# Two heads' scores in neighbouring PSUM banks, read by one instruction of 1024 columns, in the attention loop of a transformer kernel

## The chip, the cores and the metric
One core of a Trainium2 chip runs the whole program. TensorE multiplies and transposes, VectorE and ScalarE read its results out of PSUM (8 banks of 512 float32 columns in each of 128 partitions), GpSimd does small work. The metric is the device time of one execution in microseconds (us), lower is better; three runs give the median.

## The reference
Two transformer layers follow each other on x of 2 x 512 x 256: a linear attention, a mixture of 8 experts, then a softmax attention with grouped keys, and a second mixture. Each of the four parts works on a normalised x, is normalised and added to x. The change touches the third part only:

```python
# L1: 32 query heads, 8 key heads, width 8; x is viewed as batch 2, length 512 at this size
qkv = einsum('bsd,df->bsf', x, Wqkv) + bqkv
k, v = repeat(k, 4), repeat(v, 4)
scores = einsum('bqhd,bkhd->bhqk', q, k) / sqrt(8)
attn = softmax(scores, axis=-1)
out = einsum('bhqk,bkhd->bqhd', attn, v).reshape(b, s, 256) @ Wo + bo
```

## The kernel before
Every engine has its own instruction list, written out in Python, and they meet at semaphores. The attention loop works on NG = 16 groups (2 batches x 8 key heads), each with GH = 4 query heads, and each group takes TB = 4 steps of 128 rows. So there are STEPS = 64 steps c, and END = 73 turns of the loop with the drain.

The softmax needs a row's maximum before the exponentials, and the kernel makes the scores twice. In `scores1(c, i)` TensorE makes 128 queries x 512 keys per head; VectorE (`maximum`) takes each row's negated maximum into `mx`. GpSimd splits the maxima of a group into three bf16 parts and writes them as additional columns of the queries, so that the second product comes out with the maximum already subtracted. In `scores2(d, i)`, six steps later (d = c - LAG), TensorE makes 128 keys x 512 queries per head from `kT` and `qT2`, and ScalarE writes the exponentials into `pr`. `weigh(d - 2, half)` multiplies `pr` with the values into bank 6, for half of the columns at a time; the values have a column of ones that gives the sum.

A head has 32 rows of TensorE's array. Two heads of `scores1` (0, 1) and two of `scores2` (2, 3) are issued one after the other in the first half of a step, heads 2, 3 and 0, 1 in the second.

The order of a step on TensorE is `scores1(c, 0)`, `scores2(d, 0)`, `weigh(d-2, 0)`, a turn, `scores1(c, 1)`, `scores2(d, 1)`, perhaps a projection of the second batch (`project_qkv`, steps 4 to 7), `weigh(d-2, 1)`. A turn is four transposes through bank 7: at c % 4 = 0 of a finished group's output `oT` ("o"), at 1 of queries with their maxima ("q2"), at 2 of the next group's queries ("q1"), and at 3 in three of the steps of keys ("k"). ScalarE copies a turn to SBUF between its second and third exponential (q1, q2, k), or copies bank 6 to `oT` at the head of a step ahead of the "o" turn. In the first step of a group both halves of `weigh` come at the end of the step, behind `scores2(d, 1)`.

The banks: `scores1` goes round banks 0, 1, 2 (RING = 3), one head in each; `scores2` round banks 3, 4, 5. A score matmul waits until the reader has finished the bank's use three heads before: `max_read` counts VectorE's maxima, `exp_ready` ScalarE's exponentials. After step 64 only `scores2` is left, and the transposes and projection of the first batch's output (`turn_att`, `project`) are put between.

Two lines carry most of VectorE's and ScalarE's work in the loop:

```python
v.tensor_reduce(mx[n % 2][:, t, j:j + 1], s1_bank(c, j), AX.X, ALU.max, negate=True)   # L1481
nc.scalar.activation(pr[d % 3][:, j], s2_bank(d, j), ACT.Exp, scale=SCALE)              # L1256
```

On TensorE L1359 is `scores1`, L1374 `scores2`, L1389 `weigh`, L1343 a turn, L1315 a projection of queries, keys and values, L1406 and L1418 the output's transposes and projection.

Of the kernel before, what the change touches and what calls it, by code (L numbers as in the profile page):

```python
# [24 lines left out]
ALU = mybir.AluOpType  # L25
ACT = mybir.ActivationFunctionType
AX = mybir.AxisListType

P = 128
B, S, D = 2, 512, 256  # L30
NT = B * S // P
# [46 lines left out]
def build(nc, a, out):  # L78
    ctx = ExitStack()
    with ctx:  # L80
# [1058 lines left out]
        STEPS = NG * TB  # L1139
        LAG = 6  # L1140
        PROJ_AT = STEPS + 1
        PROJ_BANK = [ps[2]] * TB + ps[TB:NT]
        QKV_BANK = (4, 5, 6, 7, 3, 4, 6, 6)
        QKV_AT = 4
        RING = 3
        HEADS2 = (2, 3, 0, 1)
        AV_BANK, TURN_BANK = 6, 7

        def s1_bank(c, j):

            return ps[(c * GH + j) % RING]

        def s2_no(d, j):

            return d * GH + HEADS2.index(j)

        def s2_bank(d, j):

            return ps[RING + s2_no(d, j) % RING]

        def turns_at(c):

# [56 lines left out]
        def act_l1(act, turn_copy, complete):  # L1219
            def copy_turn(what):  # L1220
                kind, n = what
                act.wait_ge(turned, turn_no(what))
                dst = kT[n] if kind == "k" else (qT1 if kind == "q1" else qT2)[n % 2]
                nc.scalar.activation(dst[:], turn_bank(TURNS.index(what)), ACT.Copy).then_inc(turn_copied, 1)

            def hi_parts(b, t):

                act.wait_ge(qkv_ready, b * TB + t + 1)
                stack_hi(nc.scalar, b, t, "k").then_inc(k_hi_made[b], 1)
                stack_hi(nc.scalar, b, t, "q").then_inc(q_hi_made[b], 1)  # L1230

            act.wait_ge(l1_consts, L1_CONSTS)
            for t in range(TB):
                hi_parts(0, t)
            for what in FIRST:
                copy_turn(what)
            turn_copy(2, 2)
            turn_copy(2, 3)
            for c in range(END):
                d = c - LAG  # L1240
                if c == 1:
                    complete(1)
                n = (c - 12) // TB if c % TB == 0 and c >= 12 else -1
                if 0 <= n < NG:
                    act.wait_ge(av_done, (n + 1) * TB)
                    nc.scalar.activation(oT[:], ps[AV_BANK], ACT.Copy).then_inc(oT_ready, 1)
                if d >= 3 and d < STEPS:
                    act.wait_ge(av_done, d - 2)
                for i, j in enumerate(HEADS2):
                    if i == 2:  # L1250
                        for what in turns_at(c):
                            if what[0] != "o":
                                copy_turn(what)
                    if 0 <= d < STEPS:
                        act.wait_ge(s2_made, s2_no(d, j) + 1)
                        nc.scalar.activation(pr[d % 3][:, j], s2_bank(d, j), ACT.Exp, scale=SCALE).then_inc(exp_ready, 1)  # L1256
            for t in range(TB, NT):
                act.wait_ge(attT_made, t + 1)
                nc.scalar.activation(xT[:, :, t * P:(t + 1) * P],
                                     ps[t][:, 0:D].rearrange("p (c n) -> p c n", c=KC), ACT.Copy).then_inc(att1_copied, 1)  # L1260

        def pool_l1_loop(pool, link):
# [24 lines left out]
            for n in range(NG):  # L1287
                if 2 <= n < 2 + TB:
                    second_batch(n - 2)
                if n == 2 + TB:  # L1290
                    values(1)

                bb, gg = n // NKV, n % NKV
                pool.wait_ge(max_read, (n + 1) * TB * GH)
                m = mx[n % 2][:].rearrange("p t h -> p (t h)")
                low = [r[:].rearrange("p t h -> p (t h)") for r in mr]
                link(g.tensor_copy(mp[:, 0], m))  # L1297
                link(g.tensor_tensor(low[0], m, mp[:, 0], ALU.subtract))
                link(g.tensor_copy(mp[:, 1], low[0]))
                link(g.tensor_tensor(low[1], low[0], mp[:, 1], ALU.subtract))  # L1300
                link(g.tensor_copy(mp[:, 2], low[1]))
                g.tensor_copy(qs[bb][:, :, gg * GH:(gg + 1) * GH, MAXAT:MAXAT + MAXN],
                              mp[:].rearrange("p i (t h) -> p t h i", h=GH)).then_inc(max_ready, 1)

        def pe_l1(pe, turn_x):
# [3 lines left out]
            def project_qkv(t):  # L1309

                pe.wait_ge(xT_ready, 4 * 2 + t // 2 + 1)
                if t >= TB:
                    pe.wait_ge(qkv_ready, t if t == NT - 1 else TB)
                for c in range(KC):
                    last = mm(ps[QKV_BANK[t]][:, 0:QKV], xT[:, c, t * P:(t + 1) * P], wqkv[:, c],  # L1315
                              start=(c == 0), stop=(c == KC - 1))
                last.then_inc(qkv_made, 1)
# [28 lines left out]
            def scores1(c, i):  # L1346

                n, t = c // TB, c % TB
                if t == 0 and i == 0:
                    wait_read(pe, ("q1", n))  # L1350
                    wait_read(pe, ("k", n // GH))
                for j in (2 * i, 2 * i + 1):
                    k = c * GH + j
                    if k >= RING:
                        pe.wait_ge(max_read, k - RING + 1)
                    elif k == RING - 1:
                        pe.wait_ge(xT_ready, 4 * 2 + 4)
                    rows = slice(j * HW, (j + 1) * HW)
                    mm(s1_bank(c, j), qT1[n % 2][rows, t * P:(t + 1) * P], kT[n // GH][rows, :], start=True,  # L1359
                       stop=True).then_inc(s1_made, 1)  # L1360

            def scores2(d, i):

                n, kc = d // TB, d % TB
                if d == 0 and i == 0:
                    pe.wait_ge(qkv_ready, TB + 2)
                if kc == 0 and i == 0:
                    wait_read(pe, ("q2", n))
                for j in HEADS2[2 * i:2 * i + 2]:
                    k = s2_no(d, j)  # L1370
                    if k >= RING:
                        pe.wait_ge(exp_ready, k - RING + 1)
                    rows = slice(j * HW, (j + 1) * HW)
                    mm(s2_bank(d, j), kT[n // GH][rows, kc * P:(kc + 1) * P], qT2[n % 2][rows, :], start=True,  # L1374
                       stop=True).then_inc(s2_made, 1)

            def weigh(d, half):

                n, kc = d // TB, d % TB
                pe.wait_ge(exp_ready, (d + 1) * GH)  # L1380
                if half == 0 and kc == 0:
                    pe.wait_ge(vals_ready, n // NKV + 1)
                    if n == 0:
# [7 lines left out]
                if half:  # L1391
                    last.then_inc(av_done, 1)

            def turn_att(t):

                if t < TB:
                    pe.wait_ge(att_ready, NKV)
                    pe.wait_ge(max_read, GH * STEPS)
                    if t >= 2:
                        pe.wait_ge(att0_copied, t - 1)  # L1400
                    into = ps[t % 2]
                else:
                    pe.wait_ge(att_ready, NG)
                    into = ps[t]
                for c in range(KC):
                    last = nc.tensor.transpose(into[:, c * P:(c + 1) * P], xn[:, t, c * P:(c + 1) * P], ident[:])  # L1406
                last.then_inc(attT_made, 1)
# [19 lines left out]
            for c in range(END):  # L1427
# [4 lines left out]
                    scores2(d, 0)  # L1432
                if 0 <= d - 2 < STEPS and (d - 2) % TB:
                    weigh(d - 2, 0)
                for what in turns_at(c):
                    turn(what)
                if c < STEPS:
                    scores1(c, 1)
                if 0 <= d < STEPS:
                    scores2(d, 1)  # L1440
                if QKV_AT <= c < QKV_AT + TB:
# [14 lines left out]
        def dve_l1(dve, link, mark, settle, close_y, close_x):  # L1456
# [15 lines left out]
                    key_lo(t - 1)  # L1472
            key_lo(TB - 1)

            def maximum(c, j):

                n, t = c // TB, c % TB
                dve.wait_ge(s1_made, c * GH + j + 1)
                if t == 0 and j == 0 and n >= 2:
                    dve.wait_ge(max_ready, n - 1)  # L1480
                v.tensor_reduce(mx[n % 2][:, t, j:j + 1], s1_bank(c, j), AX.X, ALU.max, negate=True).then_inc(max_read, 1)  # L1481

            def outputs(n):

# [12 lines left out]
            def copy_att(t):  # L1497
                dve.wait_ge(attT_made, t + 1)
                v.tensor_copy(xT[:, :, t * P:(t + 1) * P],
                              ps[t % 2][:, 0:D].rearrange("p (c n) -> p c n", c=KC)).then_inc(att0_copied, 1)  # L1500

            for c in range(END):
                n = (c - 12) // TB if c % TB == 0 and c >= 12 else -1
                if c < STEPS:
                    for j in range(GH):
                        maximum(c, j)
                if QKV_AT <= c < QKV_AT + TB:
                    take(TB + c - QKV_AT)
                if 0 <= n < NG:
# [54 lines left out]
```

## Time and profile before

| | us |
|---|---|
| median of 3 runs (lowest, highest) | 715.25 (712.79, 715.26) |
| the profiled execution, whole time | 715.23 |
| its span from the first to the last instruction | 713.5 |
| TensorE busy in the span | 605.1 |
| VectorE, ScalarE, GpSimd busy | 398.5, 335.6, 207.2 |
| first maximum starts, last starts | 390.8, 574.5 |
| first exponential starts, last starts | 410.2, 593.6 |

The loop so takes the part of the span from about 390 to 597 us. Start times are counted from the beginning of the span. A duration of a matmul includes its way through the array, so that two matmuls one behind the other overlap in the records; the distance between starts is what one costs.

### The profile page before, as it was taken

To read this page: it belongs to the slowest core of one execution; us is meant where nothing else is said; L and a number is where in the kernel's file an instruction comes from. 1 tells how busy PE (TensorE), PEld (TensorE's weight loads), DVE (VectorE), ACT (ScalarE), POOL (GpSimd) and SP (SyncE) were. 2 spreads that over 40 slices of the span, in tenths; PEclk is the share of its full clock that TensorE was granted. 3 is DMA by queue.
4 is the path that set the end of the run, shared out by engine and by line. 5 is a ranking of instruction groups with operands and counts; after the bars stand their busy time and mean duration, and the time that the engine had idled before them with its cause. 6 is when DMAs were issued, how large, how long until landed. Compare 5 with 4: busy or idle time off the path is not lost.

```text
span 713.5 us, 11382 instructions
## 1 busy us (share of the span) xinstructions
PE 605.1 (85%) x4164; PEld 395.9 (55%) x4164; DVE 398.5 (56%) x906; ACT 335.6 (47%) x668; POOL 207.2 (29%) x307
## 2 busy tenths in 40 slices
PE   3975999999999884999916999999999998589980
PEld 2854888898788771556613444444444445246650
DVE  4331643652571485522265889889989936442225
ACT  5520432442341235222206288988988884523321
POOL 1695183074154002523333013201010101141331
PEclk9997999999999996899967699999999999699995
DMA  6000300120088009322330000000000000931213
GB/s 206 30 1 1 119 1 1 40 79 1 30 156 153 5 1 294 120 62 88 100 125 1 0 1 2 1 1 2 2 1 2 1 1 11 335 114 36 90 51 118
DMA packets 40773, 42.53 MB, mean 60 GB/s; under 512 B 7632, under 2 KB 36176, under 8 KB 40720
## 3 DMA queue, kind: packets, MB, share of 16 engines
q1 hardware_dynamic: 38512, 35.77, 17.7%
q0 software_dynamic: 2208, 6.04, 2.4%
q8 instruction: 34, 0.56, 0.3%
q14 instruction: 19, 0.16, 0.1%
HBM read 30.77 MB, written 11.03 MB: 59 GB/s over the span
## 4 chain that ended last, share of the span: by engine, by line
PE 70%; DVE 10%; POOL 7%; ACT 6%; DMA 4%; issue 2%; SPq 0%; ACTq 0%; POOLq 0%; DVEq 0%
PE psum L1359 9%; PE psum L1389 9%; PE psum L294 7%; PE psum L1085 7%; PE psum L296 7%; PE psum L295 7%; PE psum L1116 4%; PE psum L1343 4%; ACT pr L1256 3%; DVE stat L621 2%; POOL sorted_x L574 2%; PE psum L1315 2%; PE psum L938 2%; PE psum L1032 1%; PE psum L1374 1%
## 5 line engine op out<-in xcount | busy, mean ns | idle before, releaser
L1481 DVE TENSOR_REDUCE mx<-psum 128x1 f32<-128x512 f32 x256 | 158.9, 683 | 18.5 <-PE psum L1359 17.8
L1256 ACT ACTIVATE pr<-psum 128x512 f32<-128x512 f32 x256 | 138.9, 598 | 25.4 <-PE psum L1374 24.8
L1359 PE MATMUL psum<-kT,qT 32*128 32x512 f32 x256 | 81.5, 513 | 3.2 <-DVE mx L1481 1.9
L1389 PE MATMUL psum<-pr,vals 128*32 128x256 f32 x1024 | 77.9, 389 | 0.0
L1374 PE MATMUL psum<-qT,kT 32*128 32x512 f32 x256 | 66.1, 492 | 0.2 <-DVE qkv L1463 0.2
L910 ACT ACTIVATE sg<-psum 128x256 f32<-128x256 f32 x46 | 17.7, 384 | 97.3 <-PE psum L1085 62.6
L1359 PEld LDWEIGHTS psum<-kT,qT 32*128 32x128 f32 x256 | 35.3, 188 | 50.4 <-issue 23.8
L805 DVE TENSOR_TENSOR h<-sg,psum 128x256 f32<-128x256 f32 x46 | 19.3, 421 | 72.9 <-ACT sg L910 72.9
L938 PE MATMUL psum<-ident,xn_id 128*128 128x128 f32 x64 | 15.7, 406 | 49.9 <-ACT xn_id L848 49.8
L1085 PE MATMUL psum<-w_gu,xgT 128*128 x120 | 56.4, 592 | 0.0
L580 POOL DMA_INDIRECT routed_y<-yr,xg x30 | 28.9, 962 | 84.3 <-DVE yr L813 84.3
L500 POOL TENSOR_TENSOR rstd<-var,mhalf 128x4 f32<-128x4 f32 x16 | 16.8, 1051 | 108.4 <-DVE nmean L628 108.4
L1297 POOL CAST mp<-mx 128x16 bf16<-128x16 f32 x16 | 3.2, 198 | 154.6 <-DVE mx L1481 154.6
L885 ACT ACTIVATE q_hi<-q 128x512 fp32r<-128x512 f32 x32 | 20.2, 633 | 48.3 <-DVE q L747 48.3
L879 ACT ACTIVATE q<-psum 128x512 f32<-128x512 f32 x32 | 19.1, 597 | 49.9 <-PE psum L296 49.9
L938 PEld LDWEIGHTS psum<-ident,xn_id 128*128 128x128 f32 x64 | 8.7, 188 | 56.5 <-ACT xn_id L848 45.2
L552 POOL TENSOR_TENSOR ksum_t<-k_hi 128x1024 f32<-128x1024 f32 x8 | 19.2, 2395 | 69.0 <-DVE k_lo L716 69.0
L1389 PEld LDWEIGHTS psum<-pr,vals 128*32 128x32 f32 x1024 | 22.1, 108 | 29.9 <-ACT pr L1256 18.8
L294 PE MATMUL psum<-kvo_hi,q_hi 128*128 128x256 f32 x128 | 37.5, 293 | 0.7 <-DVE q_lo L695 0.7
L721 DVE TENSOR_TENSOR nk<-psum,same_head 128x8 f32<-128x8 f32 x16 | 1.9, 162 | 63.0 <-PE psum L1010 63.0
L296 PE MATMUL psum<-kvo_hi,q_lo 128*128 128x256 f32 x128 | 36.2, 283 | 0.0
L295 PE MATMUL psum<-kvo_lo,q_hi 128*128 128x256 f32 x128 | 36.2, 282 | 0.0
(201 smaller groups left out, 1386.2 us busy)
## 6 DMA issues: line engine op xcount, KB each, us to landing
w_gu<-in_L_ffn_gate_w SPq DMA_DIRECT2D x16, 256.0 KB, 6.1
w_gu<-in_L_ffn_up_w SPq DMA_DIRECT2D x16, 256.0 KB, 6.4
w_d<-in_L_ffn_down_w SPq DMA_DIRECT2D x16, 256.0 KB, 6.4
xg<-sorted_x SPq DMA_DIRECT2D x30, 128.5 KB, 2.2
sorted_x<-zeros SPq DMA_DIRECT2D x30, 128.0 KB, 5.1
wk_f<-in_L_attn_Wk SPq DMA_DIRECT2D x4, 512.0 KB, 5.1
wq_f<-in_L_attn_Wq SPq DMA_DIRECT2D x4, 512.0 KB, 5.9
wv_f<-in_L_attn_Wv SPq DMA_DIRECT2D x4, 512.0 KB, 3.7
```

What stands on the lines that cost most here:

```text
L294: nc.tensor.matmul(o, lhs[0], rhs[0], start=start, stop=False, **kw)
L295: nc.tensor.matmul(o, lhs[0], rhs[1], start=False, stop=False, **kw)
L296: return nc.tensor.matmul(o, lhs[1], rhs[0], start=False, stop=stop, **kw)
L580: g.indirect_dma_start(routed_y[l][:, :], bass.IndirectOffsetOnAxis(ap=xg[r % NXG][:, D:D + 1].bitcast(U32), axis=0), yr[r % 4][:], None). ...
L938: last = nc.tensor.transpose(ps[i if p else 4 + i][:, c * 256 + t % 2 * P:c * 256 + (t % 2 + 1) * P], xn[:, t, c * P:(c + 1) * P], ident[:])
L1085: last = mm(ps[2 + u % 2][:], xgT[r % 2][:, c], w_gu[:, bass.ds(experts[r], 1), c, :], start=(c == 0), stop=(c == KC - 1))
L1116: last = mm(ps[6 + u % 2][:, 0:D], hT[u % 2][:, c], w, start=(c == 0), stop=(c == FC - 1))
L1256: nc.scalar.activation(pr[d % 3][:, j], s2_bank(d, j), ACT.Exp, scale=SCALE).then_inc(exp_ready, 1)
L1359: mm(s1_bank(c, j), qT1[n % 2][rows, t * P:(t + 1) * P], kT[n // GH][rows, :], start=True, stop=True).then_inc(s1_made, 1)
L1374: mm(s2_bank(d, j), kT[n // GH][rows, kc * P:(kc + 1) * P], qT2[n % 2][rows, :], start=True, stop=True).then_inc(s2_made, 1)
L1389: last = mm(ps[AV_BANK][j * VW:(j + 1) * VW, cols], vals[:, n // NKV * TB + kc, n % NKV // GH * GH + j, :], pr[d % 3][:, j, cols], start=( ...
L1481: v.tensor_reduce(mx[n % 2][:, t, j:j + 1], s1_bank(c, j), AX.X, ALU.max, negate=True).then_inc(max_read, 1)
```

## The change
The scores of two heads are put side by side in two neighbouring banks, and one instruction reads both: a maximum over 128 x (2, 512), giving two columns of `mx`, and an exponential over 1024 columns. Both kinds of score share banks 0 to 5, as three pairs of banks: the list PAIRS has the pairs in TensorE's order (s1, s2, s1, s2 in a full step; only s1 in steps 0 to 5), and pair k has place k % 3 and waits until the pair last in its place has been read. Behind the last s1 the s2 pairs alternate between places 1 and 2. `max_read` and `exp_ready` count pairs. The turn is issued behind `scores1(c, 1)` instead of ahead of it, and ScalarE copies it between its two exponentials. The projection's banks 3, 4 for tiles 4, 5 become bank 6, each waiting for the addition of the tile before; the output's transposes use bank 0 alone, its projection bank 1.

```diff
-        PROJ_BANK = [ps[2]] * TB + ps[TB:NT]
-        QKV_BANK = (4, 5, 6, 7, 3, 4, 6, 6)
+        PROJ_BANK = [ps[1]] * TB + ps[TB:NT]
+        QKV_BANK = (4, 5, 6, 7, 6, 6, 6, 6)
...
-        RING = 3
-        HEADS2 = (2, 3, 0, 1)
+        HEADS1, HEADS2 = (0, 2), (2, 0)
...
+        PAIRS = []
+        for c_ in range(STEPS + LAG):
+            for i_ in range(2):
+                if c_ < STEPS:
+                    PAIRS.append(("s1", c_, i_))
+                if c_ >= LAG:
+                    PAIRS.append(("s2", c_ - LAG, i_))
+        IN_TURN = PAIRS.index(("s1", STEPS - 1, 1)) + 1
+        PLACE = [k_ % 3 if k_ < IN_TURN else 1 + (k_ - IN_TURN) % 2 for k_ in range(len(PAIRS))]
+
+        def pair_bank(what):
+
+            first = 2 * PLACE[PAIRS.index(what)]
+            return psum[:, first * 512:(first + 2) * 512]
+
+        def pair_no(step, i):
+
+            return 2 * step + i + 1
+
+        def wait_pair(pe, what):
+
+            k = PAIRS.index(what)
+            for kind, step, i in [PAIRS[k_] for k_ in range(k) if PLACE[k_] == PLACE[k]][-1:]:
+                pe.wait_ge(max_read if kind == "s1" else exp_ready, pair_no(step, i))
...
                 for i, j in enumerate(HEADS2):
-                    if i == 2:
+                    if i == 1:
                         for what in turns_at(c):
                             if what[0] != "o":
                                 copy_turn(what)
                     if 0 <= d < STEPS:
-                        act.wait_ge(s2_made, s2_no(d, j) + 1)
-                        nc.scalar.activation(pr[d % 3][:, j], s2_bank(d, j), ACT.Exp, scale=SCALE).then_inc(exp_ready, 1)
+                        act.wait_ge(s2_made, 2 * pair_no(d, i))
+                        nc.scalar.activation(pr[d % 3][:, j:j + 2].rearrange("p h n -> p (h n)"),
+                                             pair_bank(("s2", d, i)), ACT.Exp, scale=SCALE).then_inc(exp_ready, 1)
...
-                    pe.wait_ge(qkv_ready, t if t == NT - 1 else TB)
+                    pe.wait_ge(qkv_ready, t)
...
+                wait_pair(pe, ("s1", c, i))
+                for v in range(2):
+                    j = HEADS1[i] + v
                     rows = slice(j * HW, (j + 1) * HW)
-                    mm(s1_bank(c, j), qT1[n % 2][rows, t * P:(t + 1) * P], kT[n // GH][rows, :], start=True,
-                       stop=True).then_inc(s1_made, 1)
-
+                    last = mm(pair_bank(("s1", c, i))[:, v * S:(v + 1) * S], qT1[n % 2][rows, t * P:(t + 1) * P],
+                              kT[n // GH][rows, :], start=True, stop=True)
+                    last.then_inc(s1_made, 1)
...
                 if 0 <= d - 2 < STEPS and (d - 2) % TB:
                     weigh(d - 2, 0)
+                if c < STEPS:
+                    scores1(c, 1)
                 for what in turns_at(c):
                     turn(what)
-                if c < STEPS:
-                    scores1(c, 1)
                 if 0 <= d < STEPS:
                     scores2(d, 1)
...
-                v.tensor_reduce(mx[n % 2][:, t, j:j + 1], s1_bank(c, j), AX.X, ALU.max, negate=True).then_inc(max_read, 1)
+                v.tensor_reduce(mx[n % 2][:, t, HEADS1[i]:HEADS1[i] + 2],
+                                pair_bank(("s1", c, i)).rearrange("p (h n) -> p h n", h=2), AX.X, ALU.max,
+                                negate=True).then_inc(max_read, 1)
```

## Rows read from the trace of the kernel before

**Rows 1.** The page, chain that ended last: shares of the span by engine.
```profile
PE 70%; DVE 10%; POOL 7%; ACT 6%; DMA 4%; issue 2%; SPq 0%; ACTq 0%; POOLq 0%; DVEq 0%
```

**Rows 2.** Busy time by stretch: length, engines' busy us (instructions), then clock, DMA, GB/s.
```profile
393.00:396.00 3.00, 3.00 (x6) 1.32 (x6) 3.00 (x6) 1.31 (x4) 0.00 (x0) 0.50 0.00 0
...
404.00:406.00 2.00, 2.00 (x5) 0.62 (x3) 0.29 (x1) 0.00 (x0) 0.00 (x0) 0.52 0.00 0
...
486.50:497.80 11.30, 10.72 (x113) 4.96 (x116) 10.30 (x18) 10.02 (x19) 1.25 (x7) 1.00 0.01 1
```

**Rows 3.** Timeline of TensorE in one step: start, length, instructions merged.
```profile
480.10 0.66 PE L1343 MATMUL psum<-ident,qs 128*128 128x128 f32 x4
480.69 0.50 PE L1359 MATMUL psum<-kT,qT 32*128 32x512 f32 x2
480.69 0.50 PE L1374 MATMUL psum<-qT,kT 32*128 32x512 f32 x2
481.12 0.64 PE L1389 MATMUL psum<-pr,vals 128*32 128x256 f32 x8
481.69 0.77 PE L1359 MATMUL psum<-kT,qT 32*128 32x512 f32 x2
481.97 0.50 PE L1374 MATMUL psum<-qT,kT 32*128 32x512 f32 x2
```

**Rows 4.** Timelines of VectorE and ScalarE in the same group.
```profile
481.22 4.88 DVE L1481 TENSOR_REDUCE mx<-psum 128x1 f32<-128x512 f32 x8 [0.48 <-PE psum L1359]
...
482.59 2.22 ACT L1256 ACTIVATE pr<-psum 128x512 f32<-128x512 f32 x4 [0.21 <-PE psum L1374]
484.69 0.60 ACT L1246 ACTIVATE oT<-psum 128x512 f32<-128x512 f32 x1
```

**Rows 5.** Groups by form, whole span: busy us, mean ns of one, idle before.
```profile
L1481 DVE TENSOR_REDUCE mx<-psum 128x1 f32<-128x512 f32 x256 | 158.9, 683 | 18.5 <-PE psum L1359 17.8
L1256 ACT ACTIVATE pr<-psum 128x512 f32<-128x512 f32 x256 | 138.9, 598 | 25.4 <-PE psum L1374 24.8
...
L747 DVE TENSOR_TENSOR q<-q,psum 128x512 f32<-128x512 f32 x32 | 21.8, 680 | 0.6 <-PE psum L1037 0.4
...
L805 DVE TENSOR_TENSOR h<-sg,psum 128x256 f32<-128x256 f32 x46 | 19.3, 421 | 72.9 <-ACT sg L910 72.9
...
L910 ACT ACTIVATE sg<-psum 128x256 f32<-128x256 f32 x46 | 17.7, 384 | 97.3 <-PE psum L1085 62.6 <-PE psum L1078 34.7
```

**Rows 6.** The chain in order of time: a projection; output turns of five groups.
```profile
411.32 1.50 PE psum L1315 x4
...
428.48 0.63 PE psum L1343 x4
...
462.40 0.63 PE psum L1343 x4
...
474.15 0.63 PE psum L1343 x4
...
485.44 0.63 PE psum L1343 x4
...
575.78 0.63 PE psum L1343 x4
```

**Rows 7.** Timeline of TensorE, start of the loop: steps 4, 6 and 8.
```profile
402.74 2.93 PE L1315 MATMUL psum<-wqkv,xT 128*128 128x384 f32 x4
...
408.92 0.50 PE L1359 MATMUL psum<-kT,qT 32*128 32x512 f32 x2
...
417.73 1.07 PE L1389 MATMUL psum<-pr,vals 128*32 128x256 f32 x16
```

**Rows 8.** Timeline of TensorE, end of the loop, steps 65 and 66.
```profile
577.76 0.49 PE L1374 MATMUL psum<-qT,kT 32*128 32x512 f32 x2
...
581.71 0.74 PE L1374 MATMUL psum<-qT,kT 32*128 32x512 f32 x2
...
582.38 0.64 PE L1389 MATMUL psum<-pr,vals 128*32 128x256 f32 x8
```

More of the change, by code:

```diff
@@ L1141, in build @@
         PROJ_AT = STEPS + 1
-        PROJ_BANK = [ps[2]] * TB + ps[TB:NT]
-        QKV_BANK = (4, 5, 6, 7, 3, 4, 6, 6)
+        PROJ_BANK = [ps[1]] * TB + ps[TB:NT]
+        QKV_BANK = (4, 5, 6, 7, 6, 6, 6, 6)
         QKV_AT = 4
-        RING = 3
-        HEADS2 = (2, 3, 0, 1)
+        HEADS1, HEADS2 = (0, 2), (2, 0)
         AV_BANK, TURN_BANK = 6, 7
[L1149 to L1159, printed above, removed]
+        PAIRS = []
[16 more added lines that the diff above has]
+                pe.wait_ge(max_read if kind == "s1" else exp_ready, pair_no(step, i))
         def turns_at(c):
@@ L1293, in pool_l1_loop @@
                 bb, gg = n // NKV, n % NKV
-                pool.wait_ge(max_read, (n + 1) * TB * GH)
+                pool.wait_ge(max_read, (n + 1) * TB * 2)
                 m = mx[n % 2][:].rearrange("p t h -> p (t h)")
@@ L1351, in scores1 @@
                     wait_read(pe, ("k", n // GH))
[L1352 to L1357, printed above, removed]
+                if (c, i) == (0, 1):
+                    pe.wait_ge(xT_ready, 4 * 2 + 4)
+                wait_pair(pe, ("s1", c, i))
+                for v in range(2):
+                    j = HEADS1[i] + v
                     rows = slice(j * HW, (j + 1) * HW)
-                    mm(s1_bank(c, j), qT1[n % 2][rows, t * P:(t + 1) * P], kT[n // GH][rows, :], start=True,
-                       stop=True).then_inc(s1_made, 1)
+                    last = mm(pair_bank(("s1", c, i))[:, v * S:(v + 1) * S], qT1[n % 2][rows, t * P:(t + 1) * P],
+                              kT[n // GH][rows, :], start=True, stop=True)
+                    last.then_inc(s1_made, 1)
             def scores2(d, i):
                 n, kc = d // TB, d % TB
-                if d == 0 and i == 0:
-                    pe.wait_ge(qkv_ready, TB + 2)
                 if kc == 0 and i == 0:
                     wait_read(pe, ("q2", n))
[L1369 to L1372, printed above, removed]
+                wait_pair(pe, ("s2", d, i))
+                for v in range(2):
+                    j = HEADS2[i] + v
                     rows = slice(j * HW, (j + 1) * HW)
-                    mm(s2_bank(d, j), kT[n // GH][rows, kc * P:(kc + 1) * P], qT2[n % 2][rows, :], start=True,
-                       stop=True).then_inc(s2_made, 1)
+                    last = mm(pair_bank(("s2", d, i))[:, v * S:(v + 1) * S], kT[n // GH][rows, kc * P:(kc + 1) * P],
+                              qT2[n % 2][rows, :], start=True, stop=True)
+                    last.then_inc(s2_made, 1)
             def weigh(d, half):
                 n, kc = d // TB, d % TB
-                pe.wait_ge(exp_ready, (d + 1) * GH)
+                pe.wait_ge(exp_ready, (d + 1) * 2)
                 if half == 0 and kc == 0:
@@ L1392, in weigh, with wait_place0 @@
                     last.then_inc(av_done, 1)
+            def wait_place0(pe):
+                kind, step, i = [x_ for x_, at_ in zip(PAIRS, PLACE) if at_ == 0][-1]
+                pe.wait_ge(max_read if kind == "s1" else exp_ready, pair_no(step, i))
             def turn_att(t):
@@ L1397, in turn_att @@
                     pe.wait_ge(att_ready, NKV)
[L1398 to L1401, printed above, removed]
+                    pe.wait_ge(max_read, 2 * STEPS)
+                    if t:
+                        pe.wait_ge(att0_copied, t)
+                    else:
+                        wait_place0(pe)
+                    into = ps[0]
                 else:
@@ L1473, in dve_l1, with maximum @@
             key_lo(TB - 1)
-            def maximum(c, j):
+            def maximum(c, i):
                 n, t = c // TB, c % TB
-                dve.wait_ge(s1_made, c * GH + j + 1)
-                if t == 0 and j == 0 and n >= 2:
+                dve.wait_ge(s1_made, 2 * pair_no(c, i))
+                if t == 0 and i == 0 and n >= 2:
                     dve.wait_ge(max_ready, n - 1)
-                v.tensor_reduce(mx[n % 2][:, t, j:j + 1], s1_bank(c, j), AX.X, ALU.max, negate=True).then_inc(max_read, 1)
+                v.tensor_reduce(mx[n % 2][:, t, HEADS1[i]:HEADS1[i] + 2],
+                                pair_bank(("s1", c, i)).rearrange("p (h n) -> p h n", h=2), AX.X, ALU.max,
+                                negate=True).then_inc(max_read, 1)
             def outputs(n):
@@ L1499, in copy_att @@
                 v.tensor_copy(xT[:, :, t * P:(t + 1) * P],
-                              ps[t % 2][:, 0:D].rearrange("p (c n) -> p c n", c=KC)).then_inc(att0_copied, 1)
+                              ps[0][:, 0:D].rearrange("p (c n) -> p c n", c=KC)).then_inc(att0_copied, 1)
             for c in range(END):
@@ L1504, in dve_l1 @@
                 if c < STEPS:
-                    for j in range(GH):
-                        maximum(c, j)
+                    for i in range(2):
+                        maximum(c, i)
                 if QKV_AT <= c < QKV_AT + TB:
```

## The prediction
> **What bounds the kernel now.** I read the chain that ended last first: 70% of it is TensorE, 10% VectorE, 6% ScalarE [rows 1], so a microsecond taken off VectorE or ScalarE counts only where TensorE waits for it. Then the table of stretches for one group of four steps (11.30 us): TensorE is busy 10.72, VectorE 10.30 and ScalarE 10.02, at a granted clock of 1.00, TensorE's upper level of 2.4 GHz [rows 2]. Three engines are nearly full, so the order of the work decides. Last I read the timeline of one step for the prices of TensorE's pieces, start to start [rows 3]. The turn of four transposes takes 0.59 (480.10 to 480.69). The first score pair and the second start together at 480.69, on different rows of the array, and the weighing starts at 481.12, so M = 0.43 pays for four score matmuls. A half weighing is W = 0.57 (481.12 to 481.69). Then the ring shows: the second matmul of the pair at 481.69 waits for a bank, and it and the others go at 481.97, 0.28 late. A step with a turn thus needs 2M + 2W + 0.59 = 2.59 and stalls a little. Eight maxima in a row take 4.88, one 0.683, so the pitch is (4.88 - 0.68) / 7 = 0.60 [rows 4, 5]: VectorE needs 16 x 0.60 and about half a microsecond of outputs in 11.3. A plain group is 485.44 - 474.15 = 11.29; one that turns keys too, 474.15 - 462.40 = 11.75; and the 13 groups from 428.48 to 575.78 are 147.30 [rows 6].
>
> **What the change takes off.** Of 256 maxima 128 are left. Between 256 and 512 columns read from PSUM a VectorE operation grows from 421 to 680 ns, so 512 more cost 0.52: one maximum of 1024 is R = 0.683 + 0.52 = 1.20, following another at 1.12, against 1.20 for two [rows 5]. That frees 8 x 0.08 = 0.64 of VectorE per group. ScalarE's widths (384, 598) give 1.03 for an exponential of 1024 and a saving of about 0.06 a pair [rows 5]. TensorE loses no instruction. No row has a maximum of 1024: below, R can't be under 2 x 0.52 for the columns and the 0.08 that a pitch adds, 1.12; above, it is twice 0.683, 1.37. I take 1.20, by the slope.
>
> **What it adds: a wait between the two score pairs.** Pairs are written s1, s2, s1, s2, and pair k takes the place of pair k-3. So s2 of a half step waits for VectorE's maximum over the s1 of the half step before, and that whole s1 for an exponential two half steps back. From the start of an s1 its result is there 0.53 later (matmul 0.50 and a handover of 0.03: 480.69 to VectorE's start at 481.22), the maximum takes 1.20 and TensorE restarts 0.06 later. I call the sum L = 0.53 + 1.20 + 0.06 = 1.79 [rows 3, 4, 5]. While TensorE stands at s2, what is queued behind it waits too: weighing, next s1, and so VectorE's next input.
>
> **What it moves: the turn.** It now stands between the second s1 and the second s2 of the step. In [rows 3] those two share one M; with transposes between them they can't. Two matmuls alone last 0.49 as four do [rows 3, 8], so a separated pair costs a full M.
>
> I now lay out four steps, each from the start of its first s1 (a0), then first s2 (b0), second s1 (a1), second s2 (b1).
> - Steps with the q2 or q1 turn: a0 = b0 = 0; weighing; a1 = M + W = 1.00; turn 1.43 to 2.02; b1 = 2.02 (its maximum was ready at L = 1.79, hidden by the turn); next step at 2.02 + 1.00 = 3.02. The next b0 needs the second maximum, 1.00 + 1.79 = 2.79, no wait. ScalarE's copy of the turn and its exponential end 0.6 into the next step, before the s1 that reuses the place at 1.00. Two such steps: 6.04.
> - Step without a turn: a1 = 1.00, but b1 must wait until 1.79; next step at 2.79. Second maximum ends 1.73 + 1.12 = 2.85.
> - Step with the output turn and postponed weighing: a0 = 2.79, b0 = 2.91 (maximum at 2.85 and 0.06). a1 waits for the exponential of 1.79: 1.79 + 0.53 + 1.03 + 0.06 = 3.41. ScalarE copies oT (0.60) behind that exponential, starting about 0.11 before its reported end, done 3.84 [rows 4]; the turn runs 3.90 to 4.49. b1 waits for 2.79 + 1.79 = 4.58; then M and the double weighing, 1.00 (1.07 in [rows 7] with its end): next step at 6.01.
> A group is 6.04 + 6.01 = 12.05, against 11.31 before. With a key turn, T and copy k push the last part to 6.24, so 12.28 against 11.75. The last group has no q1 turn: from its output turn at 3.90 to 6.01, then 3.02 + 2.79 + 2.79, and the closing output turn at 1.11 (ScalarE's oT copy): 11.82.
>
> **The sum**, against the profiled 715.23 (span 713.50 and 1.7 around it; the median of the runs, 715.25, is the same).
> - The 13 groups: 12 x 12.05 + 2 x 0.23 + 11.82 = 156.9 against 147.30: +9.6 [rows 6].
> - From the double weighing at 417.73 to 428.48, 10.75: 1.00 + 3.02 + 3.02 + 4.19 = 11.23: +0.5 [rows 6, 7].
> - Start. Until step 6 all three pairs serve s1, so TensorE runs ahead. The clock is half (0.50 and 0.52, 1.2 GHz) until about 405.9 [rows 2], so a projection takes 2.93 there and 1.50 later [rows 6, 7]. From VectorE's 12 maxima at 1.12 and projections moved behind them I get step 6 starting at 406.7 to 408.1, not 408.92: -1.5. From there two steps with projections and the wait b1 take 9.64 to the double weighing, not 417.73 - 408.92 = 8.81: +0.8. Projection banks 3 and 4 becoming 6 costs nothing: the adding that frees bank 6 is a step old, if that cover fails it is one 0.56 addition each. Together -0.7.
> - Tail, s2 alone in two places. The second pair of a step started its two matmuls 0.24 apart before (581.71 to 582.38, 0.67 instead of 0.43) [rows 8]; a pair two places old is always read by then: 4 x -0.24 = -1.0. The one bank for the attention transposes waits for a copy one step old: nothing; without that cover 0.4 each.
> Sum: 9.6 + 0.5 - 0.7 - 1.0 = +8.4, so 723.6.
>
> **A rule against a rule.** VectorE is busy 10.30 of 11.30 us [rows 2]. The Trainium skill (Perfetto Trace Analysis, Optimizing Scalar/DVE Operations) says that grouping into larger operations helps an engine that is saturated, and that if such an engine isn't saturated but makes bubbles on others, breaking instructions up may let work finish sooner. It gives about 125 ns per VectorE access to PSUM; by that, an estimate, 8 fewer in a group would give 1.0 us in each of 14 and some 701 in all. The rows' own saving is 0.64 a group, and rival 2 prices it.
>
> **Rivals.**
> 1. The wide maximum is dearer (1.37, twice a single one). For it: no row of it over two banks. L is 1.96; the last two steps of a group grow by 0.17 twice, 0.34 x 14 = 4.8: 728.4. Chance 0.12.
> 2. VectorE is the pacemaker and is relieved: TensorE's two pairs still go together. For it: its runs of eight without a gap [rows 4]. Then a group loses 8 x 0.08 = 0.64, 14 groups 9.0: 706.3. Against it: it decides only if a maximum is read by the time TensorE wants the next s2, 1.00 after the s1; L = 1.79 would need R of 0.41. Chance 0.07.
> 3. The added waits overlap with stalls so that only the lost sharing counts. TensorE's bare order is 6.04 + (3M + 2W = 2.43) + (4M + 0.59 + 1.00 less the sharing, 2.88) = 11.35 a group, +0.04; with start and tail 714 to 716. For it: TensorE waits now too (0.28 at 481.69, 0.58 at 485.44's turn). Against it: VectorE's 1.79 lies on that order twice a group. Chance 0.10.
> My own case has 0.68; 0.03 is left for things unseen.
>
> **Numbers.** The own case reaches from R = 1.12 (2 x 0.08 x 14 = 2.2 less) and a start 3 us shorter, the part of it that hangs on the clock, which is 718.4, to a start that saves none of its 1.5 and the dear maximum, 729.9. For 8 in 10 I go down to 717. A measurement tells about 0.5% (3.6 us) from no change: slower means above 718.8. The own case lies above it but for its edge, rival 1 too: 0.81; same 0.11 (rival 3 and the edge), faster 0.08 (rival 2 and the rest).
>
> **What would show it.** In the timeline of after: in turn steps s1, turn, s2 with 1.02 from s1 to s2, and step lengths of 3.02; in a step without a turn s2's matmul idle behind VectorE with 0.79 from s1 to s2; groups of 12.05 between output turns; maxima near 1.20 and exponentials near 1.03; VectorE busy about 9.9 of 12.05, so less full than before. Wrong I would be if s2 starts with s1 also at the half steps with a turn or a wait, if the wide maximum is far from 1.2, or if the clock leaves 1.00 in the loop.

## The result: slower, and slower than forecast

The changed kernel took 736.99 us in the median (730.44 to 741.95), the kernel before 714.18 on the same chip (712.79 to 715.26). The ratio is 1.0242, with an interval of 1.0208 to 1.0277, about 731 us; it leaves out the executions more than 1.5% above the fastest of this kernel, which here are two of four, the profiled one (741.95) among them. The direction was forecast, the size not: 723.6, and 717 to 730 at the outside, lie below it.

The page of the changed kernel, first the shares of the chain that ended last, then the two groups that were widened, as in [rows 1, 5]:

```profile
PE 71%; DVE 12%; POOL 7%; DMA 4%; ACT 3%; issue 2%; SPq 0%; ACTq 0%; POOLq 0%; DVEq 0%
...
L1498 DVE TENSOR_REDUCE mx<-psum 128x2 f32<-128x1024 f32 x128 | 151.1, 1219 | 52.5 <-PE psum L1371 52.5
L1268 ACT ACTIVATE pr<-psum 128x1024 f32<-128x1024 f32 x128 | 130.8, 1024 | 44.9 <-PE psum L1383 43.3
```

A maximum of 1024 takes 1.219 (1.20 was worked out), an exponential 1.024 (1.03). VectorE's idle time in front of its maxima has grown from 18.5 to 52.5 us: it is less full, and waits for TensorE.

The timeline of TensorE in a step with a turn of queries, the step without a turn behind it, and the start of the step with the output turn (L1371 scores1, L1383 scores2, L1399 weigh, L1356 a turn), to be read against [rows 3]:

```profile
430.52 0.51 PE L1371 MATMUL psum<-kT,qT 32*128 32x512 f32 x2
430.57 0.50 PE L1383 MATMUL psum<-qT,kT 32*128 32x512 f32 x2
431.00 0.64 PE L1399 MATMUL psum<-pr,vals 128*32 128x256 f32 x8
431.57 0.50 PE L1371 MATMUL psum<-kT,qT 32*128 32x512 f32 x2
432.00 0.66 PE L1356 MATMUL psum<-ident,qs 128*128 128x128 f32 x4
432.59 0.50 PE L1383 MATMUL psum<-qT,kT 32*128 32x512 f32 x2
433.01 0.64 PE L1399 MATMUL psum<-pr,vals 128*32 128x256 f32 x8
433.58 0.50 PE L1371 MATMUL psum<-kT,qT 32*128 32x512 f32 x2
433.59 0.50 PE L1383 MATMUL psum<-qT,kT 32*128 32x512 f32 x2
434.02 0.64 PE L1399 MATMUL psum<-pr,vals 128*32 128x256 f32 x8
434.59 0.50 PE L1371 MATMUL psum<-kT,qT 32*128 32x512 f32 x2
435.44 0.49 PE L1383 MATMUL psum<-qT,kT 32*128 32x512 f32 x2 [0.34 <-DVE mx L1498]
435.86 0.64 PE L1399 MATMUL psum<-pr,vals 128*32 128x256 f32 x8
436.43 0.50 PE L1371 MATMUL psum<-kT,qT 32*128 32x512 f32 x2
436.56 0.50 PE L1383 MATMUL psum<-qT,kT 32*128 32x512 f32 x2
437.07 0.50 PE L1371 MATMUL psum<-kT,qT 32*128 32x512 f32 x2
437.65 0.63 PE L1356 MATMUL psum<-ident,oT 128*128 128x128 f32 x4
```

The order is the forecast one. In the step with the turn, s1 at 431.57 and s2 at 432.59 stand 1.02 apart, and the step is 433.58 - 430.52 = 3.06 (3.02). In the step without a turn, from 433.58 on, s2 waits for the maximum until 435.44, 0.85 behind its s1 (0.79), and the step is 2.85 (2.79).

What was not forecast is in the table of stretches (length, then busy us of TensorE, its weight loads, VectorE, ScalarE, GpSimd, then the granted clock). Two groups at the upper level, the second of them right ahead of the first fall, and two at the lower, all from output turn to output turn (the last two within 0.07):

```profile
449.84:462.05 12.21, 11.78 (x109) 5.03 (x109) 9.88 (x11) 9.55 (x12) 3.02 (x10) 1.00 0.01 2
...
474.46:486.64 12.18, 11.75 (x109) 5.03 (x109) 9.84 (x11) 9.55 (x12) 1.07 (x6) 1.00 0.01 1
...
486.64:505.60 18.96, 18.96 (x109) 7.13 (x110) 9.87 (x11) 9.95 (x12) 1.35 (x7) 0.51 0.00 0
...
544.55:563.39 18.84, 18.84 (x109) 7.07 (x110) 9.86 (x11) 9.95 (x12) 1.35 (x7) 0.51 0.00 1
```

Twice TensorE's clock fell from 2.4 to 1.2 GHz inside the loop (0.51), for 23.8 us each (486.9 to 510.7, 544.9 to 568.7), where the trace of the kernel before has 1.00 from 406 us to the end of the loop. Such a group takes 6.6 to 6.7 us more, and the next one, in which the clock comes back, 2.3 more: about 9 us a fall. A third fall, from 602.9 to 606.4, lies behind the last s1, in the drain.

### The profile page after: what moved, and what is told of

Same layout as the page of the kernel before. It is cut to its first block, busy times and chain, and to the rows that moved or that the text cites. A ratio compares the mean times of both kernels' runs of the same rounds, so it can differ in the third digit from the quotient of the medians.

```text
span 739.7 us, 11126 instructions
## 1 busy us (share of the span) xinstructions
PE 633.1 (86%) x4164; PEld 398.7 (54%) x4164; DVE 391.5 (53%) x778; ACT 329.2 (45%) x540; POOL 206.8 (28%) x307
## 4 chain that ended last, share of the span: by engine, by line
PE 71%; DVE 12%; POOL 7%; DMA 4%; ACT 3%; issue 2%; SPq 0%; ACTq 0%; POOLq 0%; DVEq 0%
PE psum L1399 10%; PE psum L294 7%; PE psum L1085 7%; PE psum L296 7%; PE psum L295 7%; PE psum L1371 7%; PE psum L1383 5%; PE psum L1356 4%; PE psum L1116 4%; DVE mx L1498 3%; DVE stat L621 2%; POOL sorted_x L574 2%; PE psum L1328 2%; PE psum L938 1%; PE psum L1032 1%
## 5 line engine op out<-in xcount | busy, mean ns | idle before, releaser
L1498 DVE TENSOR_REDUCE mx<-psum 128x2 f32<-128x1024 f32 x128 | 151.1, 1219 | 52.5 <-PE psum L1371 52.5
L1268 ACT ACTIVATE pr<-psum 128x1024 f32<-128x1024 f32 x128 | 130.8, 1024 | 44.9 <-PE psum L1383 43.3
L1399 PE MATMUL psum<-pr,vals 128*32 128x256 f32 x1024 | 88.7, 437 | 0.0
L1383 PE MATMUL psum<-qT,kT 32*128 32x512 f32 x256 | 70.0, 542 | 6.1 <-DVE mx L1498 5.8
L1371 PE MATMUL psum<-kT,qT 32*128 32x512 f32 x256 | 68.7, 548 | 3.7 <-DVE mx L1498 2.0
L1371 PEld LDWEIGHTS psum<-kT,qT 32*128 32x128 f32 x256 | 25.5, 201 | 60.7 <-issue 34.9
L1399 PEld LDWEIGHTS psum<-pr,vals 128*32 128x32 f32 x1024 | 23.6, 116 | 35.1 <-issue 27.5
L1383 PEld LDWEIGHTS psum<-qT,kT 32*128 32x128 f32 x256 | 26.0, 198 | 23.7 <-DVE mx L1498 16.1
```

Source lines behind the costliest of these rows:

```text
L1268: nc.scalar.activation(pr[d % 3][:, j:j + 2].rearrange("p h n -> p (h n)"), pair_bank(("s2", d, i)), ACT.Exp, scale=SCALE).then_inc(exp_re ...
L1371: last = mm(pair_bank(("s1", c, i))[:, v * S:(v + 1) * S], qT1[n % 2][rows, t * P:(t + 1) * P], kT[n // GH][rows, :], start=True, stop=True)
L1383: last = mm(pair_bank(("s2", d, i))[:, v * S:(v + 1) * S], kT[n // GH][rows, kc * P:(kc + 1) * P], qT2[n % 2][rows, :], start=True, stop=True)
L1399: last = mm(ps[AV_BANK][j * VW:(j + 1) * VW, cols], vals[:, n // NKV * TB + kc, n % NKV // GH * GH + j, :], pr[d % 3][:, j, cols], start=( ...
L1498: v.tensor_reduce(mx[n % 2][:, t, HEADS1[i]:HEADS1[i] + 2], pair_bank(("s1", c, i)).rearrange("p (h n) -> p h n", h=2), AX.X, ALU.max, neg ...
```

## The experiments

Each ran beside the kernel before. "Group" is the distance of two output turns without a key turn, at the clock of 1.00.

**The changed kernel again.** No edit.

> The changed kernel unchanged, in several executions. Theory 'order and clock': at full clock a plain group of four steps takes 12.2 us (turn steps 3.02, the step without a turn 2.85), and beyond that each execution has one or two stretches of some 22 us in the loop where the granted clock is 0.50, each worth about 9 us: times near 722, 731 or 740 for none, one or two stretches, and nothing between. Rival 'order alone': the low stretches belonged to that one execution, and most executions show 722. Rival 'instructions': the wide maximum or exponential is slower in some executions, then their durations differ between runs.

Measured: 730.55, 737.3, 728.65, 742.2, 740.67, 731.77; the group 12.19. In the profiled execution (730.55) the low stretches were short ones:

```profile
486.00:490.00 4.00, 3.94 (x29) 1.70 (x29) 2.21 (x4) 1.85 (x2) 0.44 (x3) 0.57 0.00 0
490.00:500.00 10.00, 9.57 (x88) 4.14 (x85) 8.02 (x7) 8.05 (x10) 1.03 (x6) 0.99 0.00 0
500.00:503.00 3.00, 3.00 (x21) 1.11 (x20) 1.86 (x4) 1.49 (x2) 0.22 (x1) 0.50 0.03 5
```

A third like them is at 513 to 517, and each costs its group 1.45 (13.64 instead of 12.19); a fourth, from 588.7 to 595.4, is in the drain. So the times are not three levels, as I had expected: the falls differ in number and in length. The wide maximum is 1219 ns here too, which refutes the rival of slower instructions, and no execution came near 722; the lowest is 728.65.

**The turn ahead again**, all else of the change kept.

```diff
-                if c < STEPS:
-                    scores1(c, 1)
                 for what in turns_at(c):
                     turn(what)
+                if c < STEPS:
+                    scores1(c, 1)
```

> The changed kernel with the turn put back ahead of the second scores1 of the step. Theory 'the maximum's way sets the order': laid out by the same waits the group comes to 2.86 + 3.38 + 2.91 + 3.22 = 12.4 us, a little above 12.2, since the second s1 comes later and the next step's s2 waits for its maximum. Rival 'the lost sharing at the turn is the cost': s1 and s2 of the second half start together again, and a group falls to 11.4. If the clock falls because pairs run alone, it should fall less here.

Measured: 735.9 (729.51 to 737.84), ratio 1.0256 (1.0211 to 1.030). The group was 12.70, beyond the 12.4 expected, and far from 11.4: the second s1 comes later, and more s2 wait.

```profile
444.21 0.50 PE L1371 MATMUL psum<-kT,qT 32*128 32x512 f32 x2
445.12 0.50 PE L1383 MATMUL psum<-qT,kT 32*128 32x512 f32 x2 [0.41 <-DVE mx L1498]
...
447.70 0.50 PE L1371 MATMUL psum<-kT,qT 32*128 32x512 f32 x2
448.54 0.50 PE L1383 MATMUL psum<-qT,kT 32*128 32x512 f32 x2 [0.34 <-DVE mx L1498]
```

With shared pairs the moved turn is a gain of 0.5 a group. The lost sharing at the turn is not the whole cost. In the profiled execution (737.7) the clock stayed at 1.00 through all 13 groups, but behind their last output turn it was 0.50 from 593.0 to 606.6.

**Maxima over half of the keys.** VectorE reads 256 of each 512 columns; the softmax is then shifted by another number.

```diff
-  pair_bank(("s1", c, i)).rearrange("p (h n) -> p h n", h=2), AX.X
+  pair_bank(("s1", c, i)).rearrange("p (h n) -> p h n", h=2)[:, :, 0:S // 2], AX.X
```

> The changed kernel, but each maximum reads only the first 256 of the 512 columns of its two heads (the maxima are over half of the keys; all else is done), so that it lasts near 0.68 instead of 1.22. Theory 'the wait of s2 for the maximum': L falls from 1.8 to 1.27, the step without a turn from 2.8 to 2.3, the group from 12.2 to 11.4, turn steps stay at 3.02; 10 us less at equal clock. Rival 'TensorE's order alone': the group stays near 12.2. On the clock: if the waits at s2 make it fall, it stays at 1.00 here and the time is near 712; if the lone pairs do, it falls as before and the time is near 720 to 729.

Measured: 712.94 (711.23 to 714.79), ratio 0.9971 (0.9952 to 0.999). The maximum took 0.691, the group 11.55, and the clock stayed at 1.00 through all 13 groups; one short fall (573.7 to 577) lies behind their last output turn. Its step without a turn, in the timeline:

```profile
440.86 0.51 PE L1371 MATMUL psum<-kT,qT 32*128 32x512 f32 x2
...
441.87 0.50 PE L1371 MATMUL psum<-kT,qT 32*128 32x512 f32 x2
442.17 0.50 PE L1383 MATMUL psum<-qT,kT 32*128 32x512 f32 x2
442.60 0.64 PE L1399 MATMUL psum<-pr,vals 128*32 128x256 f32 x8
443.17 0.50 PE L1371 MATMUL psum<-kT,qT 32*128 32x512 f32 x2
```

It takes 2.31 instead of 2.85. With the shorter maximum 0.64 of the 0.88 that a group had grown by is gone (12.19 - 11.55), so it comes by way of the maximum. The kernel is no version to keep, since its maxima leave out half of each row.

**The kernel before with only the turn moved** behind the second scores1 (the edit of the turn-ahead run, reversed, in single banks).

> The kernel before with only the turn moved behind the second scores1, single banks and 512 columns kept. Theory 'what the move costs by itself is small': turn steps go from 2.96 to 3.02, and the output turn no longer waits 0.5 for oT; the group stays within 0.2 of 11.3, the time within 3 us of before, if the clock stays at 1.00. Rival 'the move is the cost': three lost sharings of 0.43 a group, group 12.4, 14 us and more. If the lone pairs bring the clock down, low stretches appear here too, each 9 us.

Measured: 736.55 (735.18 to 740.59), ratio 1.0301 (1.0264 to 1.0338). I had this wrong. The group is 12.72 at a clock of 1.00, and the move by itself costs more than the whole change does at that clock. Of the 22.5 us by which its span is longer, 18.4 are the 13 groups; 4.4 are the start, where the clock stayed at 0.50 until 410.8 instead of 405.8.

```profile
478.46 0.66 PE L1343 MATMUL psum<-ident,qs 128*128 128x128 f32 x4
479.05 0.49 PE L1374 MATMUL psum<-qT,kT 32*128 32x512 f32 x2
479.47 0.64 PE L1389 MATMUL psum<-pr,vals 128*32 128x256 f32 x8
480.04 0.50 PE L1359 MATMUL psum<-kT,qT 32*128 32x512 f32 x2
480.05 0.74 PE L1374 MATMUL psum<-qT,kT 32*128 32x512 f32 x2
480.71 0.64 PE L1389 MATMUL psum<-pr,vals 128*32 128x256 f32 x8
481.28 0.53 PE L1359 MATMUL psum<-kT,qT 32*128 32x512 f32 x2
481.74 0.66 PE L1343 MATMUL psum<-ident,ks 128*128 128x128 f32 x4
```

Turn to turn is 3.28. Besides the lost sharing (0.43), the pair at 480.05 takes 0.67 instead of 0.43, because ScalarE copied the turn before its last two exponentials and the ring of three isn't free yet. I had assumed that stalls of before would absorb the move.

**Two instructions a pair.** The changed kernel, each pair read by two instructions of 512 columns and released behind the second.

```diff
+                for u in range(2):
+                    j = HEADS1[i] + u
+                    last = v.tensor_reduce(mx[n % 2][:, t, j:j + 1], pair_bank(("s1", c, i))[:, u * S:(u + 1) * S], AX.X,
+                                           ALU.max, negate=True)
+                last.then_inc(max_read, 1)
```

> The changed kernel with its three shared pairs, but each pair is read by two instructions of 512 columns on VectorE and on ScalarE, the pair being released behind the second. Theory 'banks and order cost, width hardly matters': L grows from 1.85 by 0.06, the group from 12.19 to about 12.3, the time by 1 to 2 us at equal clock. Rival 'the wide instruction is the cost': the group falls toward 11.3. Rival 'width carries the gain': the group rises by 8 x 0.08 or more, to 12.8.

ScalarE's exponentials were split in the same way. Measured: 748.5, 747.86, 728.25, 748.13, too far apart for a ratio; in the profiled one (748.5) the group is 12.45 where the clock is 1.00, and there are low stretches from 466 to 511 and from 582 to 586 us. The width is worth 0.26 a group: more than the 0.1 I expected, less than the 0.64 of the rival. It is a gain, too small for the order's cost. The pair was still released as a whole here; no run releases each half by itself.

**Waits filled.** To see what makes the clock fall, additional transposes of the identity into the free bank 7.

```diff
+  def filler(c, count):
+      wait_read(pe, [x_ for c_ in range(c) for x_ in turns_at(c_)][-1])
+      for t in range(count):
+          nc.tensor.transpose(ps[TURN_BANK][:, t * P:(t + 1) * P], ident[:], ident[:])
...
+  if 12 <= c < STEPS and c % TB == 0:
+      filler(c, 1)
   if c < STEPS:
       scores1(c, 1)
+  if 8 <= c < STEPS and c % TB == 3 and not turns_at(c):
+      filler(c, 2)
+  if 12 <= c < STEPS and c % TB == 0:
+      filler(c, 1)
   for what in turns_at(c):
       turn(what)
```

> The changed kernel with transposes of the identity into the free bank 7 while TensorE would stand: two behind the second s1 of a step without a turn, one ahead of and one behind the second s1 of a step with an output turn. They are additional work of 0.15 us each, 4 in a group, in waits of 0.41, 0.2 and 0.15. Theory 'the falls of the clock follow TensorE's waits ahead of an output turn': the group at full clock stays at 12.2 (at most 0.15 more), no stretch of the loop is below 1.00, the times lie together near 722 to 725. Rival 'the falls hang on the pairs that run alone in half of the array': the falls stay, times 729 to 742 as before.

Measured: 723.89 (722.52 to 725.2), ratio 1.012 (1.0096 to 1.0144), the group 12.31, the clock at 1.00 from 408 us to the end of the loop in the profiled execution. The kernel does more work and is 7 us and more faster than the change unedited (about 731, 728.65 at the least), which was not timed beside it. But the group had another length, so two runs took the edit apart.

**Only the two in the step without a turn.**

> Of the four additional transposes only the two in the step without a turn are left; they lie whole in a wait of 0.41, so the group keeps its length of 12.19, unlike in the run before, where it was 12.31. Theory 'the wait brings the clock down': no stretch of the loop below 1.00 or only short ones, times near 722 and close together. Rival 'it was the new length of the group against the chip's looking that helped': the length is the old one, so the falls come back and the times spread from 728 to 742.

Measured: 722.88 (721.2 to 728.47), ratio 1.0132 (1.0097 to 1.0166), the group 12.19 as in the change, no fall in the loop of the profiled execution. One of the six took 728.47, at a mean clock of 0.930 where the others have 0.935 to 0.939, so a fall seems to be rarer now, not impossible. In the timeline the transposes (L1413) lie in the old wait:

```profile
446.77 0.50 PE L1371 MATMUL psum<-kT,qT 32*128 32x512 f32 x2
447.20 0.44 PE L1413 MATMUL psum<-ident 128*128 128x128 f32 x2
447.61 0.50 PE L1383 MATMUL psum<-qT,kT 32*128 32x512 f32 x2
```

**Only the two in the step with an output turn.**

> Only the two single transposes in steps with an output turn are left, the wait of 0.41 in the step without a turn stays open. The group is 12.31 long, as with all four. Theory 'the wait brings the clock down': the falls come back, at least in some executions, 728 and more. Rival 'the length of the group helped': no falls, times near 724.

Measured: 726.5 (725.48 to 727.45), ratio 1.0167 (1.0141 to 1.0194), the group 12.31, and one short low stretch:

```profile
427.00:439.00 12.00, 11.66 (x110) 4.95 (x109) 9.70 (x11) 9.39 (x12) 2.72 (x10) 1.00 0.01 1
439.00:442.00 3.00, 3.00 (x20) 1.66 (x23) 2.05 (x4) 1.70 (x2) 2.12 (x6) 0.51 0.00 0
```

A fall came back, though a short one: neither expectation fits whole. The length of the group isn't the remedy, since the run before this had the old length and no fall. But against the 742 of the next run, on the same chip, these two transposes gained 15 us with the wait of 0.41 left open: most of the effect doesn't hang on that wait.

**The control on the same chip.**

> The changed kernel unchanged, as a control on the same chip as the filled ones: times from 728 to 742 with falls of the clock in the loop.

Measured: 741.98 (736.24 to 743.14), ratio 1.036 (1.0323 to 1.0396), the group 12.2, falls at 487 and 545 again. Against it, two transposes a group that lie in a wait are worth 19 us. None of the 16 executions of the unedited change, in three sets, took less than 728.65.

**A third row group beside the second s1.**

```diff
+                if i == 1 and 8 <= c:
+                    wait_read(pe, [x_ for c_ in range(c) for x_ in turns_at(c_)][-1])
+                    mm(ps[TURN_BANK], qT1[n % 2][0:HW, t * P:(t + 1) * P], kT[n // GH][0:HW, :], start=True, stop=True)
```

> The changed kernel with one more score matmul beside each second s1 from step 8 on, for a head of another row group, into the free bank 7 (its result is not used). It runs at the same time as the pair and adds no length, and TensorE's waits stay: the group stays at 12.2, but a pair that was alone has a third row group at work. Theory 'the open wait in the step without a turn brings the clock down': the falls stay, times 728 to 743. Rival 'the half empty array of the lone pairs does': no falls in the loop, times near 722.

Measured: 724.09 (722.7 to 729.47), ratio 1.0157 (1.0126 to 1.0189), the group 12.20, no fall in the loop of the profiled execution. Two of the six took 728.73 and 729.47, at mean clocks of 0.930 and 0.927 where the others have 0.934 to 0.938, so again the falls are rarer, not gone. The unedited change was not timed beside this one. About the same three us in three kernels, first the profiled execution of the change, then the third step filled, then this one:

```profile
484.00:487.00 3.00, 2.57 (x21) 1.24 (x20) 2.51 (x3) 2.31 (x4) 1.09 (x6) 0.98 0.00 0
487.00:490.00 3.00, 3.00 (x21) 0.96 (x19) 1.79 (x4) 1.43 (x2) 0.16 (x1) 0.50 0.00 0
```
```profile
484.00:487.00 3.00, 2.91 (x24) 1.42 (x22) 2.51 (x3) 2.31 (x4) 1.15 (x6) 1.00 0.00 0
487.00:490.00 3.00, 3.00 (x34) 1.14 (x32) 2.54 (x5) 2.05 (x3) 0.11 (x1) 1.00 0.00 0
```
```profile
484.00:487.00 3.00, 2.58 (x22) 1.01 (x21) 2.52 (x3) 2.31 (x4) 0.83 (x4) 1.00 0.00 0
487.00:490.00 3.00, 3.00 (x34) 1.34 (x34) 2.54 (x5) 2.06 (x3) 0.42 (x2) 1.00 0.00 0
```

The first and the third are busy for the same time (2.57 and 2.58) and wait for the same, yet only the first loses its clock. My theory of the wait falls with this: additional work at the same busy time did as much as work put into the wait. That it is the share of the array at work that counts would fit both, but it isn't shown, since both edits also add instructions and weight loads.

**The start by itself**: the kernel before, with six banks for scores1 in steps 0 to 5 and projections 4 and 5 in bank 6.

```diff
-            return ps[(c * GH + j) % RING]
+            return ps[(c * GH + j) % (2 * RING if c < LAG else RING)]
```

> The kernel before (single banks, 512 columns, turn ahead), but in steps 0 to 5, where there is no scores2 yet, scores1 goes round all six banks, and projections 4 and 5 use bank 6. Theory 'the start is the part of the change that gains': the changed kernel came to its first double weighing 2.8 us sooner counted from the first scores; here 2 to 3 us sooner, all groups at 11.3, time 712 to 713, faster than both. Rival 'the gain at the start came from the wide maxima': 24 maxima save only 12 x 0.07 there, the time is then within 0.5 us of before, or the projections waiting for bank 6 cost it.

> The kernel before with six banks for scores1 in steps 0 to 5, once more. Its first profile had the output turn of step 12 at 425.5 instead of 428.5 and a span 3.0 us shorter, but its executions averaged 0.9988 of before. Theory 'a real gain of the start, partly blurred': the ratio lies between 0.996 and 0.999 again. Rival 'nothing in the mean': 1.000.

Measured: 713.83 against 714.83, ratio 0.9988 (0.9966 to 1.001), and 713.73 against 714.64, 0.9986 (0.997 to 1.0002). In both profiled executions the output turn of step 12 came 36.7 and 36.8 us behind the first turn of queries, against 39.6 before, and the groups were 11.3. In the mean about 1 us is left, which this measurement can't tell from nothing. No version here that does all of the work is shown to beat the kernel before.

## Why the prediction was wrong, step by step

The step that failed is the sum, by a term that it did not have: behind the start every price stood at the granted clock of 1.00, because the loop of before shows 1.00 and TensorE would be no idler. "If the clock leaves 1.00 in the loop" stood there as a way to be wrong, but no rival and no price, though [rows 2] show the lower level in the same kernel. Measured, this term is the way from 722.9 to 731 or 742, 8 to 19 us; the 19 are from two kernels timed side by side. With the falls prevented at the same group length the kernel takes 722.9, and 723.6 was forecast. That these two lie so close is partly luck: in the table the groups are 1.8 dearer than forecast and the start 2.0 cheaper.

The other terms can be held against the execution with the third step filled (span 721.0, against 713.5), which has the order of the change and in the loop a clock of 1.00:

| term | forecast | measured |
|---|---|---|
| 13 groups, output turn of step 12 to that of 64 | +9.6 | 158.74 - 147.30 = +11.4 |
| start, from the first score matmul to that turn | -0.2 | 36.11 - 38.26 = -2.2 |
| tail, to the last output turn | -1.0 | 20.89 - 21.81 = -0.9 |
| ahead of the loop, behind it | 0 | -0.9, 0 |
| sum | +8.4 | +7.5 |

- Added wait of s2 for the maximum: right in place; L is 1.85 instead of 1.79 and comes in twice a group, which makes 0.12 of the 0.14 between 12.05 and 12.19. The half maxima show that this way carries at least 0.64 of the growth of 0.88.
- Turn moved: right that sharing is lost in turn steps (3.02 to 3.06). But the lost sharing is not what the move is worth, as I had taken it for: with single banks it costs 1.41 a group, in shared pairs it gains 0.5. A two by two: single banks 11.31 ahead and 12.72 behind, shared pairs 12.70 and 12.19.
- Width: 0.26 a group by the run with two instructions. Rival 1 (dear maximum) is out, 1.219 and not 1.37.
- Start: mis-sized. Step 6 began 14.53 behind the first scores instead of 18.70, 4.2 sooner and not 1.5: the clock was back at 401.5, before the second projection (1.46; the first took 2.93), while I let it stay low until 405.9. The two steps after gave 1.4 back, 0.8 had been worked out. When the clock comes back differs between executions: from the first score matmul to the output turn of step 12 the seven profiled ones with the order of the change take 36.1 to 37.2.
- Rival 2, VectorE as pacemaker, is out: it waits 52.5 us. Rival 3 (11.35) comes nearer to the half maxima, 11.55, than to the change. Which of the two rules of the Trainium skill that the prediction sets against each other holds here is not settled: an instruction broken in two made the group longer by 0.26, and none was tried that lets TensorE go on sooner.

What stays open is why the clock falls. It kept its level in the moved-turn kernel with single banks (group 12.72, no fall in the profiled execution) and through the 13 groups of the profiled turn-ahead kernel (12.70), though both do the same matmuls in a longer time. All falls seen in the loop of the unedited change begin at an output turn, behind the step in which the wait and the lone pairs lie closest, but not at each one, and I have no rule that says which.

## What to carry to other kernels

Before sharing a ring between two engines, write down for one round who releases each buffer to whom: in a shared ring the next stage's matmul can come to wait for the other stage's reader. Here that way cost 0.64 a group and more, and the wider instruction gave 0.26 back. Look at what runs beside what on TensorE when a piece is moved; matmuls that used different rows of the array at the same time are cheap only together. And give the clock a rival with a price when an edit rearranges TensorE's work; two idle transposes in a wait told here, in one run against the unedited kernel, how much of the time was the clock's.

## What the hardware showed unexpectedly

TensorE lost its upper clock level right behind a group in which its records were busy 11.75 of 12.18 us, a larger share than the kernel before has (10.72 of 11.30 [rows 2]), and in which its longest wait was 0.34 us. The Trainium skill (TensorE: Matmul & The Clock Gate, HAM oscillation — how this bites in real kernels) tells of such falls where the engine waits for its data between batches of matmuls; here there was no such stand. One more matmul on a third group of 32 rows beside each lone pair, with the group busy 11.77 of 12.19 us, kept the level in the profiled execution. Busy time in the records alone thus doesn't tell whether the clock will hold. And one VectorE instruction over two neighbouring banks cost about what its columns cost: 1.219 for 1024 against 0.683 for 512, so 0.54 for 512 more, where the one-bank rows gave 0.52.
